# A two-layer gather-and-mix kernel: first group's products on raw fp32 operands, a third x buffer, later bias tables, scores in two split passes, and softmax rows scaled on ScalarE

## What is computed

```python
attn_in = tanh(einsum('bsd,da->bsa', x, W1) + b1)          # W1: 512 x 128
scores  = einsum('bsa,a->bs', attn_in, v)
mask    = where(pt == 0, l <= j, where(pt == 1, l >= j, l != j))
p       = softmax(where(mask, scores[:, None, :], -1e30), axis=-1)
x       = x + einsum('bjl,bld->bjd', p, x) / cnt           # cnt: allowed entries in row j
out     = x + einsum('bsd,bdh->bsh', x, W[cat_ids]) + b[cat_ids]
```

## Time and profile before

| | us |
|---|---|
| median of 3 runs (335.58 to 336.35) | 335.98 |
| the profiled execution's own time | 336.02 |
| its span, first to last instruction | 334.2 |
| PE busy | 317.1 (95%) |
| DVE busy | 293.0 (88%) |
| ACT busy | 257.0 (77%) |
| DMA, mean rate over the span | 304 GB/s |

### The profile page before, as it was taken

The page is one execution under the profiler, slowest core; times in us unless marked ns, Lnnn a source line. Parts: engine busy times, 40 slices in busy tenths (PEclk is TensorE's granted clock), DMA queues, the critical chain, the costliest instruction groups (busy, mean ns, idle before and its releaser), DMA issues.

```text
span 334.2 us, 4766 instructions
## 1 busy us (share of the span) xinstructions
PE 317.1 (95%) x1416; PEld 251.7 (75%) x1416; DVE 293.0 (88%) x305; ACT 257.0 (77%) x373; POOL 4.7 (1%) x19
## 2 busy tenths in 40 slices
PE   7475899999999999999999999999999999999996
PEld 5253678787887878787887878787887878788784
DVE  1559969898998989898998989899998989899860
ACT  2468378796978879696978879697887879697843
POOL 5000000000000000000000000000000000000000
PEclk9969699999999999999999999999999999999999
DMA  6999777998989799898989899898979899784113
GB/s 151 349 424 421 271 297 267 363 328 251 402 289 420 234 373 345 281 381 259 416 267 387 299 370 349 305 351 272 393 261 394 296 335 375 279 273 176 63 63 126
DMA packets 21642, 101.56 MB, mean 304 GB/s; under 512 B 2706, under 2 KB 2706, under 8 KB 11634
## 3 DMA queue, kind: packets, MB, share of 16 engines
q1 hardware_dynamic: 21458, 100.94, 82.5%
q0 software_dynamic: 160, 0.33, 1.0%
HBM read 84.48 MB, written 16.78 MB: 303 GB/s over the span
## 4 chain that ended last, share of the span: by engine, by line
PE 89%; DMA 4%; DVE 3%; SPq 2%; issue 1%; ACT 0%; DVEq 0%
PE ps_y L507 17%; PE ps_y L509 17%; PE ps_y L508 17%; PE ps_pre L474 13%; PE ps_y L522 4%; PE ps_y L520 4%; PE ps_y L519 4%; PE ps_y L521 4%; DMA w_raw<-in_L_cond_W 4%; PE ps_scores L482 4%; PE ps_pT L495 2%; DVE w_lo L363 1%; PE ps_scores L484 1%; DVE xT_lo L350 1%; DVE w_raw L339 1%
## 5 line engine op out<-in xcount | busy, mean ns | idle before, releaser
L363 DVE TENSOR_TENSOR w_lo<-w_raw,w_hi 128x2048 fp32r<-128x2048 f32 x63 | 143.9, 2285 | 0.0
L255 ACT ACTIVATE w_hi<-w_raw 128x2048 fp32r<-128x2048 f32 x63 | 121.9, 1935 | 4.2 <-DVE w_raw L339 4.2
L507 PE MATMUL ps_y<-w_hi,xT_hi 128*128 128x512 f32 x256 | 104.2, 407 | 5.2 <-DVE w_lo L356 5.2
L509 PE MATMUL ps_y<-w_hi,xT_lo 128*128 128x512 f32 x256 | 101.2, 395 | 0.0
L508 PE MATMUL ps_y<-w_lo,xT_hi 128*128 128x512 f32 x256 | 100.6, 393 | 0.0
L507 PEld LDWEIGHTS ps_y<-w_hi,xT_hi 128*128 128x128 f32 x256 | 48.6, 190 | 14.7 <-DVE w_lo L356 5.6
L509 PEld LDWEIGHTS ps_y<-w_hi,xT_lo 128*128 128x128 f32 x256 | 48.6, 190 | 11.2
L508 PEld LDWEIGHTS ps_y<-w_lo,xT_hi 128*128 128x128 f32 x256 | 48.8, 191 | 9.7
L391 DVE TENSOR_TENSOR z_lo<-ps_y,z_hi 128x512 fp32r<-128x512 f32 x64 | 43.7, 684 | 6.0 <-ACT z_hi L283 6.0
L283 ACT ACTIVATE z_hi<-ps_y 128x512 fp32r<-128x512 f32 x64 | 39.4, 616 | 9.4 <-PE ps_y L509 9.4
L339 DVE TENSOR_TENSOR w_raw<-w_raw,ident 128x512 f32<-128x512 f32 x63 | 43.0, 683 | 3.4 <-DMA w_raw<-in_L_cond_W 3.4
(11 more groups left out here) (64 smaller groups left out, 257.7 us busy)
## 6 DMA issues: line engine op xcount, KB each, us to landing
w_raw<-in_L_cond_W SPq DMA_DIRECT2D x63, 1024.0 KB, 7.9
out<-out_sb SPq DMA_DIRECT2D x64, 256.0 KB, 6.6
x_raw<-in_x SPq DMA_DIRECT2D x15, 1024.0 KB, 10.5
x_raw<-in_x SPq DMA_DIRECT2D x2, 512.0 KB, 6.1
w_raw<-in_L_cond_W SPq DMA_DIRECT2D x2, 512.0 KB, 10.0
w_raw<-in_L_cond_W SPq DMA_DIRECT2D x1, 256.0 KB, 7.1
b_raw<-in_L_cond_b POOLq DMA_DIRECT2D x2, 128.0 KB, 8.5
type_all<-in_itok_B POOLq DMA_DIRECT2D x1, 32.0 KB, 6.9
```

What stands on the lines that cost most here:

```text
L255: nc.scalar.activation(w_hi[k % NH][:], w_raw[k % NW][:], ACT.Copy).then_inc(w_hi_ready, 1)
L363: nc.vector.tensor_tensor(w_lo[k % NL][:], w_raw[k % NW][:], w_hi[k % NH][:].bitcast(F32), ALU.subtract).then_inc(w_lo_ready, 1)
L507: nc.tensor.matmul(y[:], xT_hi[q][:, c, xs], w_hi[k % NH][:, c, :], start=(c == 0), stop=False)
L509: last = nc.tensor.matmul(y[:], xT_lo[q][:, c, xs], w_hi[k % NH][:, c, :], start=False, stop=(c == DC - 1))
```

## The change

- Group 0's products (`hidden`, `xw` of samples 0 to 3) and `hidden(1)` use the raw fp32 tiles directly, one native product per chunk instead of three split passes. `xw_raw` still waits for the identity to be added. No hi or lo copy is made of matrices 0 to 3 and of x of group 0.
- x gets a third raw buffer (`NX` 3), its split copies keep two (`NT`). x of group 2 is loaded in the head.
- x of group 0 is loaded in one piece. W1, b1 and v are loaded by ACT's queue, before its first operation. POOL loads the 64 mask kinds into one partition first (DVE makes `type_row` from that); the spread kinds after the first half of matrix 0 has landed, the spread categories and the bias tables after matrix 2 has landed.
- Scores: ACT makes `av_hi` = attn times v in fp32r, DVE `av_lo` = attn times v minus `av_hi`, and PE adds two passes against a matrix of ones in place of the one unsplit product.
- The scaling of `probs` moves from one DVE instruction behind `row_scale_group` to four ACT instructions at b = 0, behind `z_hi`. In ACT's loop `copy_out` moves behind tanh and the exponentials.
- 26 warm-up products instead of 40. `one_hot` and `b_both` are made with fewer instructions.
- The head is written out by hand on each engine up to sample 4, where the loop begins.

The core of the diff (left out: declarations, the setup arithmetic on DVE, and bodies that stay):

```diff
@sync
             def load_w(k):
                 cat = sp.value_load(cat_row[0:1, k:k + 1], min_val=0, max_val=C - 1)
-                if k >= NW:
+                if k - NW >= RAW:
                     sp.wait_ge(w_lo_ready, w_count(k - NW))
+                elif k >= NW:
+                    sp.wait_ge(xw_done, k - NW + 1)
...
             def load_x(g):
-                if g >= NX:
-                    sp.wait_ge(xT_lo_ready, x_count(g - NX))
+                if g == NX:
+                    sp.wait_ge(xw_done, RAW)
+                elif g > NX:
+                    sp.wait_ge(xT_lo_ready, g - NX)
+                    sp.wait_ge(pre_done, g - NX + 1)
...
             load_w(1)
+            load_w(2)
             load_x(1)
-            load_w(2)
             load_w(3)
             load_w(4)
-            for t in range(-2, B + 3):
+            load_w(5)
+            load_x(2)
+            load_w(6)
+            for t in range(B + 3):
@gpsimd
+            pool.wait_ge(w0_in[0], 16)
+            pool.dma_start(type_all[:], types.rearrange("(a n) -> a n", a=1).to_broadcast([P, B]))\
+                .then_inc(types_in, 16)
+            pool.wait_ge(w_in[2], 16)
             pool.dma_start(cat_all[:], cats.rearrange("(a n) -> a n", a=1).to_broadcast([P, B]))\
                 .then_inc(cat_all_in, 16)
@scalar
                 nc.scalar.activation(attn[:], ps_pre[:], ACT.Tanh, bias=b1_col[:]).then_inc(attn_ready, 1)
+                act.wait_ge(attn_ready, g + 1)
+                nc.scalar.activation(av_hi[:], attn[:], ACT.Copy, scale=v_col[:]).then_inc(av_hi_ready, 1)
...
+            def scale_group(g):
+                act.wait_ge(scale_ready, g + 1)
+                for i in range(G):
+                    last = nc.scalar.activation(probs[:, i, :], probs[:, i, :], ACT.Copy, scale=row_scale[:, i:i + 1])
+                last.then_inc(probs_ready, 1)
...
+            tanh_group(0)
             act.wait_ge(w1_in, 16)
             nc.scalar.activation(w1_hi[:], w1_raw[:], ACT.Copy).then_inc(w1_hi_ready, 1)
+            split_z_hi(0)
+            exp_group(0)
+            split_z_hi(1)
+            scale_group(0)
+            split_xT_hi(1)
+            split_mix_hi(0)
             act.wait_ge(b_low_in, 16)
             act.wait_ge(b_high_in, 16)
+            nc.scalar.activation(b_both[:], b_raw[:], ACT.Copy).then_inc(b_hi_ready, 1)
+            tanh_group(1)
+            split_w_hi(4)
+            split_z_hi(2)
+            split_w_hi(5)
+            for k in range(G, B + 3):
                 g, b = k // G, k % G
+                if k <= B:
                     split_z_hi(k - 1)
+                if k == G:
+                    exp_group(1)
+                    copy_out(0)
+                    split_w_hi(6)
+                if b == 0 and g < GROUPS:
+                    scale_group(g)
+                if b == 1 and g < GROUPS:
                     split_mix_hi(g)
                 if b == 2 and g + 1 < GROUPS:
                     tanh_group(g + 1)
                 if b == 3 and g + 1 < GROUPS:
                     exp_group(g + 1)
+                copy_out(k - 3)
+                if b == 0 and g + 1 < GROUPS:
+                    split_xT_hi(g + 1)
                 if k + 3 < B:
                     split_w_hi(k + 3)
@vector
+            def split_av_lo(g):
+                dve.wait_ge(av_hi_ready, g + 1)
+                nc.vector.scalar_tensor_tensor(av_lo[:], attn[:], v_col[:], av_hi[:].bitcast(F32),
+                                               ALU.mult, ALU.subtract).then_inc(av_lo_ready, 1)
...
+            add_identity(4)
+            split_av_lo(1)
+            split_w_lo(4)
+            split_z_lo(2)
+            add_identity(5)
+            max_group(1)
+            split_w_lo(5)
+            add_identity(6)
+            row_scale_group(1)
...
+                if b == 2 and g + 1 < GROUPS:
+                    split_av_lo(g + 1)
+                split_z_lo(k - 1)
+                if k == G:
+                    add_identity(7)
@tensor
+            def hidden_raw(g):
+                if g == 0:
+                    pe.wait_ge(w1_in, 16)
+                else:
+                    pe.wait_ge(attn_ready, g)
+                pe.wait_ge(x_in[g], 16)
+                for c in range(DC):
+                    last = nc.tensor.matmul(ps_pre[:], w1_raw[:, c, :], x_raw[g][:, c, :],
+                                            start=(c == 0), stop=(c == DC - 1))
+                last.then_inc(pre_done, 1)
...
-                nc.tensor.matmul(ps_scores[:], v_col[:].to_broadcast([P, P]), attn[:], start=True, stop=False)
+                nc.tensor.matmul(ps_scores[:], ones[:], av_hi[:], start=True, stop=False)
+                pe.wait_ge(av_lo_ready, g + 1)
+                nc.tensor.matmul(ps_scores[:], ones[:], av_lo[:], start=False, stop=False)
...
+            warm_up(26)
+            hidden_raw(0)
+            xw_raw(0)
+            scores_group(0, kinds)
+            xw_raw(1)
+            xw_raw(2)
+            transpose_probs(0)
+            hidden_raw(1)
+            xw_raw(3)
+            scores_group(1, kinds)
+            pe.wait_ge(bias_ready, 2)
+            pz(0)
+            pz(1)
+            for k in range(G, B + 2):
```

More of the change, by code:

```diff
@@ L50, in program @@
         x_raw = [sb(f"x_raw{i}", [P, DC, GS], F32) for i in range(NX)]
-        xT_hi = [sb(f"xT_hi{i}", [P, DC, GS], F32R) for i in range(NX)]
-        xT_lo = [sb(f"xT_lo{i}", [P, DC, GS], F32R) for i in range(NX)]
+        xT_hi = [sb(f"xT_hi{i}", [P, DC, GS], F32R) for i in range(NT)]
+        xT_lo = [sb(f"xT_lo{i}", [P, DC, GS], F32R) for i in range(NT)]
         w_raw = [sb(f"w_raw{i}", [P, DC, D], F32) for i in range(NW)]
@@ L59, in program @@
         attn = sb("attn", [P, GS], F32)
+        av_hi = sb("av_hi", [P, GS], F32R)
+        av_lo = sb("av_lo", [P, GS], F32R)
         probs = sb("probs", [P, G, S], F32)
@@ L193, in _ @@
                     store(t - 3)
[L194 removed]
+                if b == 3 and g + 3 < GROUPS:
                     load_x(g + 3)
@@ L433, in _ @@
-            add_identity(3)
-            for k in range(B + 1):
+            dve.wait_ge(setup_step, 4)
+            nc.vector.scalar_tensor_tensor(one_hot[:], cat_all[:], row_f[:, 2:3], cat_high[:],
+                                           ALU.is_equal, ALU.add).then_inc(bias_ready, 1)
+            add_identity(4)
[6 more added lines that the diff above has]
+            add_identity(6)
@@ L436, in _ @@
+            row_scale_group(1)
+            for k in range(G, B + 1):
                 g, b = k // G, k % G
-                if k == 0:
-                    max_group(0)
                 if b == 3 and g + 1 < GROUPS:
@@ L496, in transpose_probs, with xw_raw @@
                 last.then_inc(probsT_done, 1)
+            def xw_raw(k):
+                for c in range(DC):
+                    if k == 0 and c % HALF == 0:
+                        pe.wait_ge(wi_ready, c // HALF + 1)
+                    elif k >= 1 and c == 0:
+                        pe.wait_ge(wi_ready, wi_count(k))
+                    last = nc.tensor.matmul(ps_y[k][:], x_raw[0][:, c, k * S:(k + 1) * S], w_raw[k][:, c, :],
+                                            start=(c == 0), stop=(c == DC - 1))
+                last.then_inc(xw_done, 1)
             def xw(k):
[L499 removed]
+                y, xs, q = ps_y[k % NY], slice((k % G) * S, (k % G + 1) * S), (k // G) % NT
                 if k >= NY:
                     pe.wait_ge(out_ready, k - NY + 1)
[L502 to L503 removed]
+                pe.wait_ge(w_lo_ready, w_count(k))
+                if k == RAW:
+                    pe.wait_ge(xT_lo_ready, 1)
                 for c in range(DC):
[L505 to L506 removed]
                     nc.tensor.matmul(y[:], xT_hi[q][:, c, xs], w_hi[k % NH][:, c, :], start=(c == 0), stop=False)
```

212 lines of the change are left out of this document (80 added, 132 removed).

## The result

The changed kernel takes 324.11 us (median; 323.57 to 324.44) against 335.88 (335.58 to 336.35): a ratio of 0.9647, 95% interval 0.9629 to 0.9665, or 11.8 us. The forecast was 327.0 in a range of 321.5 to 332.5. The profiled execution took 323.99 us, 1.8 over its span, as before.

What follows compares the result with a forecast made beforehand. PE was taken to bound the loop, DVE close behind. Span 334.2 - 4.5 (head) - 5.2 (scores) + 0.7 (loop loss) = 325.2 us, plus 1.8 outside the span: 327.0 us, range 321.5 to 332.5 (inner 324 to 329.5).

Steps and rivals of the forecast that it cites:

- The bound: Loop: PE, busy all 260.0 us from 60 to 320 us, sets the 19.00 us period; DVE is runner-up at 18.1.
- The scores, -0.40 per group: Loop, PE: scores go from 0.86 to 0.46 us, leaving a period of 18.60; -5.2 us over 13 groups.
- ACT and DVE additions: Loop, per group: av_hi 0.6 us and four scalings 1.1 on ACT, av_lo 0.60 on DVE; ACT 17.7, DVE 18.1.
- The laid-out group: One loop group: DVE loses 0.4 us to xT_hi, DVE and PE level, 0 to 0.1 lost per group; 0.7 in all.
- Rival C: Loop: DVE and ACT become the bound, period stays at 19.0, total 331.5 us; chance 0.16.
- The head, -4.5 forecast: Start to the end of group 2's scores: 58.8 us instead of 63.3, -4.5 us (ends -2 and -9).
- The chain that was written down: Head, ACT and DVE: from add_identity(4) at 31.7 to the scaling of group 1 at 45; PE waits 5.6 us.
- The half clock: Head, behind the wait before group 1's transposes: group 2's scores end at 59.3 us, against 57.5 at full clock.
- Rival B: Head: PE gap stays short and clock full, gain 9 us with all 5.2 of the loop; 321.8 us, chance 0.18.
- Rival D: Head: raw products open at half clock after the warm-up and the chip stays there; 329.5 to 330 us, chance 0.10.
- Rival E: Loop: scaling on ACT makes the transposes wait in every group, 18 us, total 345; chance 0.06 together with Rival F.
- Rival F: Head: raw operands cost more than the two-pass row; double price adds 20 us of PE; chance 0.06 with Rival E.

Runs made afterwards that it cites:

- e1: Changed kernel with the old unsplit scores product, no av_hi or av_lo: 328.27 us, ratio 0.9765 to the kernel before.
- e3: Changed kernel with ACT's copy_out moved behind xT_hi (b = 0) and w_hi (b = 3) from step 7 on: 322.65 us.
- e10: Changed kernel with the old first loads: x of group 0 in halves around W1 on SP, v and b1 on SP: 326.95 us.
- e11: Changed kernel with 36 unused warm-up products in PE's wait before the transposes of group 1: 323.52 us.
- e6: Changed kernel without the 26 warm-up products: 326.21 us.
- e12: e9 with av_lo(2) put ahead of w_lo(8) on DVE: 319.06 us, ratio 0.9487 to the kernel before.
- e4: Changed kernel with the head's instructions reordered on ACT and DVE, scaling of group 1 and xT_hi(2) ahead of w_hi(6) on ACT: 322.02 us.
- e9: Changed kernel with both new orders, that of e3 in the loop and that of e4 in the head: 321.17 us.

## Why the prediction was right, point by point

- **The bound** held: PE sets the loop while its period is above DVE's. e1 shows it.
- **The scores, -0.40 per group:** 18.60 is the measured PE period (e3, and groups 3 and 4 of after to 0.02).
- **ACT and DVE additions.** In the timeline of after:

```profile
51.17 0.73 ACT L272 ACTIVATE av_hi<-attn,v_col 128x512 fp32r<-128x512 f32 x1
...
51.80 0.58 ACT L306 ACTIVATE out_sb<-ps_y 128x512 f32<-128x512 f32 x1
...
39.83 1.26 ACT L286 ACTIVATE probs<-probs,row_scale 128x128 f32<-128x128 f32 x4
...
40.99 0.58 ACT L306 ACTIVATE out_sb<-ps_y 128x512 f32<-128x512 f32 x1
...
52.37 0.74 DVE L383 SCALAR_TENSOR_TENSOR av_lo<-attn,v_col,av_hi 128x512 fp32r<-128x512 f32 x1
...
53.03 0.68 DVE L405 TENSOR_TENSOR z_lo<-ps_y,z_hi 128x512 fp32r<-128x512 f32 x1
```

av_hi steps by 0.63 (51.17 to 51.80; taken 0.6 with its wait), four scalings by 1.16 (39.83 to 40.99; taken 1.1), av_lo by 0.66 (52.37 to 53.03; taken 0.60, inside the bounds). The estimate of 1.17 for four scalings from the Trainium skill (ScalarE: Activation LUTs, What ACT_TABLE_LOAD costs) agrees with the 1.16 of the trace.
- **The laid-out group** was the step that paid: it forecast 0.4 us of DVE waiting for xT_hi (0.45 measured) and DVE and PE level, with 0 to 0.1 us lost per group. The loss is 0.16 in 11 of the 13 groups, some 1.8 us in all, where 0.7 was put in. Two parts of it were missing: av_lo's 0.06, and a wait that I had not seen, 0.18 us for w_hi behind row_scale. Together they are 0.24, more than was missing, so the other steps of the layout were somewhat too long. Rival C (all 5.2 us lost) did not come, because of 0.24 us.
- **The head, -4.5 forecast, -8.7 measured.** The mechanism was right: a PE wait before the transposes of group 1, on ACT's scaling, 5.6 forecast and 5.26 measured. The chain that was written down, w_hi(4) to the scaling, was put at 13.3 us (31.7 to 45) and took 13.4 (27.66 to 41.10 in the chain above). What failed is the term ahead of it, the arrival of the data, which opened the chain 4.0 us too late. I took the landings of before and shifted them by bytes at 420 GB/s: hidden(0) at 9, scores(1) done at 33. It was 6.80 and 30.1. Matrix 2, put at 20, had landed when POOL went on at 16.25, and the bias tables, put at 29 to 30, let ACT go on at 25.20:

```profile
25.20 0.63 ACT L324 ACTIVATE b_both<-b_raw 128x512 fp32r<-128x512 f32 x1 [1.82 <-DMA b_raw<-in_L_cond_b]
```

  The rows that I shifted come from a head in which the DMA engines moved 137 and 346 GB/s in the two halves of the first 16 us; after has 199 and 428. By 16 us that is 5.0 MB against 3.9, and the 1.1 MB between them are 2.6 us at 420 GB/s. e10, with the old issue of the first loads, starts hidden(0) at 8.70, near the 9 of the forecast; so the issue, which I took over unchanged in its effect, makes 1.9 us of the 4.0, and the range of 8 to 9.7 left the case out. What brought matrix 2 in early by the rest is not shown. Behind the transposes the path to the end of the scores of group 2 took 13.4 us instead of the 14.2 laid out at half clock, since the clock came back after 4.66 us and not after 6.1.
- **The half clock** was priced at 1.8 us (59.3 against 57.5); e11 shows 0.75.
- **Rival B** had 9 us of gain in the head, close to the 8.7 measured, but not for this reason: the PE gap did not stay short and the clock did not stay full. Its 5.2 us from the loop did not come.
- **Rival D** (raw products open at half clock) did not happen: the gap behind the warm-up was 0.93 us, because the data came early. e6 gives its price, 2.1 us, and e10, with a gap of 1.90 us, has part of it.
- **Rival E** (transposes wait in every group): PE has no such wait in the loop; it appears only once in e12, at group 2. Rival F: hidden(0) took 3.67 us and xw(0) 3.60, two passes of 0.43 per product, as the row of the scores said.
- The two errors, -4.2 us in the head and +1.2 in the loop, have opposite signs; the total was off by 2.9 us. That 324.11 still falls into the inner range of 324 to 329.5 is luck: with the loop as forecast it would have been 1.2 us lower.

## What to carry to other kernels

Lay out one period of a loop that two engines share nearly evenly, instruction by instruction from the sync point, before moving work between them: here the sum of the queues said "fits", and the order on ACT took back what the move gave, until copy_out went behind the copies that DVE waits for. Where a kernel changes from one form of its operands to another, look at the first units in the new form: their preparation has no lead there, and the order in which the side engines take it was worth 5 us here (from 324.1 to 319.1, with the loop order). A landing time taken over from another head holds only as long as the loads in front of it are issued in the same way.

## What the runs showed of the hardware

- The profile's clock row does not tell of the start. In e6_warm0 the first eight raw passes take 6.40 us, in after 3.67, and the row of that stretch says 1.00:

```profile
6.54:12.94 6.40, 6.40 (x9) 2.82 (x10) 1.42 (x6) 0.00 (x0) 0.57 (x1) 1.00 1.00 384
...
6.54 6.40 PE L498 MATMUL ps_pre<-x_raw,w_raw 128*128 128x512 f32 x8 [6.54 <-DMA x_raw<-in_x]
```

- A native fp32 product (128 x 128 by 128 x 512) was two passes, 0.43 to 0.44 us apart at full clock, in all 24 raw products of after; a pass of split operands took 0.23 us from start to start.
- The same PE wait of 2.03 us for av_lo(2) left the clock at full in e4 (the pass behind it took 0.50 us) and was followed by half pace in e9 (0.80 us). The wait of 1.90 us in e10 was followed by half pace, one of 1.98 us in before, ahead of the pass at 9.41 us, was not (0.50 us). So the length of the wait alone does not tell.
- The DMA engines, busy for the same share of about 1.0, moved different amounts from 8 to 16 us: 346 GB/s (before), 365 (e10, at a share of 0.95) and 428 (after). These kernels differ in the loads issued by then; which of the moved loads makes the difference, v and b1 of 0.5 KB each among them, stays open.
